# Attention in front of a mixture of experts: row maxima over two PSUM banks, masks written by TensorE, seven PSUM banks dealt out anew

## The reference

```
x1  = layernorm(x)
q, k, v = split(x1 @ W_qkv.T + b_qkv)          # 16 heads, head_dim 8
logits  = where(causal, q @ k.T * 8**-0.5, -inf)
x = x + softmax(logits) @ v @ W_proj.T + b_proj
```

```
z = layernorm(x); top_vals, top_idx = top_k(z @ Wg, 2); gate = softmax(top_vals)
for e in range(8):
    a = gelu(layernorm(z, ln_w[e], ln_b[e]) @ fc1_w[e] + fc1_b[e])
    out += (a @ fc2_w[e] + fc2_b[e]) * comb[:, e]
x = x + out
```

## Time and profile before

| what | value |
|---|---|
| median of three runs | 540.32 us |
| span of the profiled execution | 560.3 us |
| busy: PE, DVE, ACT, POOL | 473.9, 373.1, 322.9, 366.1 us |
| stretch with both passes running | about 40 to 345 us |
| period of one batch in it | 43.1 us (the same rows recur at 173.33, 216.43 and 259.51 us) |
| experts' part | about 368 to 560 us |

### The profile page before, as it was taken

The page is one execution under the profiler, slowest core; times in us unless marked ns, Lnnn a source line. Parts: engine busy times, 40 slices in busy tenths (PEclk is TensorE's granted clock), DMA queues, the critical chain, the costliest instruction groups (busy, mean ns, idle before and its releaser), DMA issues.

```text
span 560.3 us, 11807 instructions
## 1 busy us (share of the span) xinstructions
PE 473.9 (85%) x3296; PEld 277.1 (49%) x3296; DVE 373.1 (67%) x1316; ACT 322.9 (58%) x661; POOL 366.1 (65%) x712
## 2 busy tenths in 40 slices
PE   3379999999999998998898988786992999999930
PEld 1134443543443453443444443364981888888920
DVE  4588878889889889889889997741543521222226
ACT  2137786776676776676676666752550555565610
POOL 5956676586986986987887876955556444445520
PEclk9589999999999999999999999897996899999985
DMA  2323133134233234234224212276642685666439
GB/s 62 93 57 105 65 93 109 58 105 118 68 101 117 78 87 129 73 91 130 75 66 130 71 40 79 79 236 213 219 159 86 213 264 180 216 194 187 154 129 328
DMA packets 52726, 70.83 MB, mean 126 GB/s; under 512 B 11063, under 2 KB 38430, under 8 KB 52662
## 3 DMA queue, kind: packets, MB, share of 16 engines
q1 hardware_dynamic: 47478, 59.19, 34.7%
q0 software_dynamic: 4320, 8.53, 4.5%
q10 hardware_dynamic: 864, 2.36, 1.2%
HBM read 36.49 MB, written 20.94 MB: 102 GB/s over the span
## 4 chain that ended last, share of the span: by engine, by line
PE 51%; DVE 17%; issue 8%; POOL 6%; SPq 5%; DMA 4%; another core or an unknown queue 4%; ACT 3%; ACTq 0%; DVEq 0%; POOLq 0%
PE acc_bank L748 10%; PE slots L739 10%; PE slots L648 7%; PE acc_bank L680 7%; PE slots L665 5%; SPq L496 4%; DVE masked L940 3%; PE misc L616 3%; POOL z_dram L1235 2%; DVE z L893 2%; DVE row_max L934 2%; POOL probs L1252 2%; DMA y_in<-y_dram 2%; PE slots L644 2%
## 5 line engine op out<-in xcount | busy, mean ns | idle before, releaser
L811 ACT ACTIVATE probs<-slots 128x512 f32<-128x512 f32 (+1 forms) x352 | 185.6, 562 | 86.0 <-PE slots L665 79.2
L940 DVE CUSTOM_DVE_ANT_0 masked<-slots,causal_row 128x512 bf16<-128x512 f32 (+1 forms) x256 | 148.9, 614 | 20.8 <-PE slots L648 20.7
L648 PE MATMUL slots<-stack_k,stack_q 125*128 125x256 bf16 (+3 forms) x512 | 128.5, 307 | 19.4 <-DVE row_max L940 7.5
L1252 POOL TENSOR_SCALAR_AFFINE_SELECT probs<-probs 128x128 f32<-128x128 f32 (+2 forms) x352 | 116.1, 350 | 41.3 <-ACT probs L811 37.4
L665 PE MATMUL slots<-stack_q,stack_k 128*128 128x256 bf16 (+3 forms) x512 | 125.6, 301 | 2.9 <-DVE row_max L934 1.5
L1282 POOL DMA_INDIRECT y_dram<-y,z_in x71 | 69.7, 982 | 73.4 <-DVE y L1126 56.8
L841 ACT ACTIVATE hidden<-slots,w_in 128x256 f32<-128x256 f32 (+1 forms) x156 | 63.1, 455 | 82.6 <-PE acc_bank L748 29.2
L680 PE MATMUL acc_bank<-probs,v 128*32 128x512 f32 (+3 forms) x1024 | 95.6, 447 | 3.4 <-POOL probs L1252 2.7
L648 PEld LDWEIGHTS slots<-stack_k,stack_q 125*128 125x128 bf16 x512 | 48.3, 99 | 95.4 <-DVE row_max L940 49.7
L1235 POOL DMA_INDIRECT z_dram<-z,pos x64 | 63.6, 994 | 32.1 <-DVE pos L1034 17.7
L748 PE MATMUL acc_bank<-hidden,w_in 128*128 128x256 f32 (+1 forms) x312 | 73.0, 376 | 7.8 <-issue 4.0
(11 more groups left out here) (168 smaller groups left out, 523.1 us busy)
## 6 DMA issues: line engine op xcount, KB each, us to landing
w_in<-in_wpack SPq DMA_DIRECT2D x39, 516.0 KB
o_dram<-oT SPq DMA_DIRECT2D x32, 256.0 KB, 2.3
stack_k<-parts SPq DMA_DIRECT2D x95, 64.0 KB
stack_q<-parts SPq DMA_DIRECT2D x93, 64.0 KB
z_in<-z_dram SPq DMA_DIRECT2D x32, 132.0 KB
xt<-in_x SPq DMA_DIRECT2D x8, 256.0 KB, 3.7
onT<-o_dram SPq DMA_DIRECT2D x8, 256.0 KB
o_inv<-inv_dram SPq DMA_DIRECT2D x8, 256.0 KB
```

The costliest lines, as they stand in the source:

```text
L648: mm = pe.matmul(cols[:, i, :], q[0:K1, hh, blk * P:blk * P + P], k[0:K1, hh, 0:w], start=len(heads) == 1, stop=True, skip_group_check=True)
L811: act.activation(probs_of(n), columns(n, slot), ACT.Exp, scale=SCALE).then_inc(s_exp, 1)
L940: dve.tensor_tensor_reduce(out=masked[:, n % MASKED, 0:w], in0=slots[:, slot, 0:w], in1=causal_row[:, T - w:T], scale=1.0, scalar=NEG, op0 ...
L1252: pool.affine_select(out=diag, in_=diag, compare_op=ALU.is_ge, fill=0.0, base=0, pattern=[[0, len(heads)], [1, P]], channel_multiplier=-1) ...
```

## The change

**Pass 1** is cut into six pieces per group in place of eleven: two heads of four blocks over two banks (2 x 512 columns) twice, two heads of three blocks over two banks (2 x 384) twice, four heads of two blocks over two banks (2 x 512), and four heads of one block in one bank (512). They stand at ticks 0, 2, 4, 6, 8 and 10. Every piece gets its mask from TensorE and its maxima from one `tensor_reduce`; the fused instruction, its accumulator read and `causal_row` are gone.

**PSUM**: four banks (`scores`) belong to pass 1, used as two pairs; three (`banks`) are a ring that pass 2 and all that was in `misc` share in the order of the list; `acc_bank` stays.

**The probability masks** are cut by GpSimd for two units at once, at ticks 1, 3, 5, 7, 9 and 10 of the unit count, six instructions per group in place of eleven. `probs` has one slot per unit of a group, and exp waits for the p-by-v matmul of the group before.

The core of the diff (renamings of `misc[...]` to `misc(stage)[...]` and of the experts' banks are left out):

The list and the banks:

```diff
+LARGEST = tuple((blocks, tuple(range(h, h + n))) for blocks, n in ((4, 2), (3, 2), (2, 4), (1, 4))
+                for h in range(0, HPG, n))
+SCORED = len(LARGEST)
+SCORE_AT = (0, 2, 4, 6, 8, 10)
+CUT_AT = (1, 3, 5, 7, 9, 10)
+CUT_OF = (2, 4, 5, 6)
...
-SLOTS = 6
+RING = 3
...
-        if n < G * UNITS:
-            add(("pass1", n))
+        g, tick = divmod(n, UNITS)
+        if g < G and tick in SCORE_AT:
+            add(("pass1", SCORED * g + SCORE_AT.index(tick)))
...
+    ring = [s for s in schedule if s[0] == "pass2" or s[0] in MISC]
+    last_pass2 = ring.index(("pass2", G * UNITS - 1))
+    for i, s in enumerate(ring):
+        bank_of[s] = i % RING if i <= last_pass2 else RING - 1
+        used_before[s] = last_use.get(bank_of[s])
+        last_use[bank_of[s]] = s
...
-        slots = ctx.enter_context(nc.psum_tensor("slots", [P, SLOTS, 512], F32))
+        scores = ctx.enter_context(nc.psum_tensor("scores", [P, 4, 512], F32))
+        banks = ctx.enter_context(nc.psum_tensor("banks", [P, RING, 512], F32))
         acc_bank = ctx.enter_context(nc.psum_tensor("acc_bank", [P, 512], F32))
-        misc = ctx.enter_context(nc.psum_tensor("misc", [P, 512], F32))
...
+        def wait_bank(eng, stage):
+
+            before = used_before[stage]
+            if before and before[0] == "pass2":
+                wait(eng, s_exp, before[1] + 1)
+            elif before:
+                wait(eng, s_free, misc_no[before] + 1)
```

TensorE's claim of a bank, its pass 1, and the wait ahead of a p-by-v stage:

```diff
             def claim(stage):
 
-                wait(pe, s_free, misc_no[stage])
+                if stage != ("k", 0):
+                    wait(pe, s_free, misc_no[stage])
+                wait_bank(pe, stage)
...
+            def pass1(m):
+                g, u, w, heads, per_bank = largest_of(m)
                 b, hg = divmod(g, NG)
+                wait(pe, s_max, m - 1)
...
-                if len(heads) > 1:
-                    pe.matmul(cols[:, :, w - P:w], ident_b[:, :], causal[:, 0:len(heads), :],
+                for cols in used:
+                    pe.matmul(cols[:, :, w - P:w], ident_b[:, :], causal[:, 0:per_bank, :],
                               start=True, stop=False, skip_group_check=True)
...
-                last = g * UNITS + ROW_END[row]
-                wait(pe, s_cut, last + 1)
+                wait(pe, s_cut, len(CUT_AT) * g + CUT_OF[row])
```

ScalarE's wait before an exp, VectorE's maxima, and GpSimd's cut:

```diff
-                if n >= P_RING:
-                    old_g, old_u = divmod(n - P_RING, UNITS)
-                    row = NT - UNIT[old_u][0]
-                    wait(act, s_pv, NT * old_g + PV_ORDER.index(row) + 1)
+                if g > 0:
+                    wait(act, s_pv, NT * (g - 1) + PV_ORDER.index(NT - w // P) + 1)
...
-                    dve.tensor_tensor_reduce(out=masked[:, n % MASKED, 0:w], in0=slots[:, slot, 0:w],
-                                             in1=causal_row[:, T - w:T], scale=1.0, scalar=NEG, op0=ALU.add, op1=ALU.max,
-                                             accum_out=largest).then_inc(s_max, 1)
+                used = scores[:, 2 * (m % 2):2 * (m % 2) + len(heads) // per_bank, 0:per_bank * w]
+                if per_bank > 1:
+                    used = used.rearrange("p b (h w) -> p (b h) w", w=w)
+                dve.tensor_reduce(largest, used, AX.X, ALU.max).then_inc(s_max, 1)
...
+                if u not in CUT_AT:
+                    return
                 wait(pool, s_exp, n + 1)
-                diag = probs_of(n)[:, :, 0:P]
+                if len(heads) < HPG:
+                    diag = probs[:, u - 1:u + 1, 0:len(heads) * w]
```

137 lines of the change are left out of this document (64 added, 73 removed).

## The result

Four runs of the changed kernel took 546.7 to 550.75 us, median 548.4; the kernel before beside them 540.61. The ratio is 1.0139 [1.0119, 1.0160], in brackets its 95% interval. Forecast were 536.4 and a range that ended at 546. The profiled execution took 547.7 us with a span of 545.6, so 2 us lie around the span.

A forecast was written before the change was run, and what follows sets the result against it. TensorE bounds the light stretch; in full periods TensorE and VectorE, nearly equal, hold each other up. Periods -6.0, light groups +2.9, first groups -0.9 sum to -4.0, times 0.964 -3.9: 536.4 us; range 526 to 546, the forecast's own 533 to 540.

The forecast's parts named there:

- Masks: Pass 1's two-head pieces: eight added mask matmuls a group at 56 ns, +0.44 us a group, +13.1 us of TensorE's work.
- rival C: Pass 1's masks cost as much as a weight load: 238 x 43 ns = +10, 546 us; chance 0.06.
- Row maxima: VectorE's maxima in pass 1 fall from 6.13 to 5.70 us a group: 0.43 less, 1.7 a batch.
- Cuts: GpSimd's probability cuts fall from 3.86 to 2.90 us a group; the chain to `rstd` ends 0.9 us earlier.
- How PE and DVE mesh: Attention, per batch: TensorE 40.2 us, VectorE 36.8; stalls fall from 4.7 to 1.7, period 41.9, 1.2 less.
- the gaps "by `z`": TensorE's gaps by the layer norm, recorded as 0.22 and 0.17 us, ending with VectorE; 0.2 left as a stall.
- Fill: First two groups, pass 1 alone: VectorE sets the pace, so 2 x 0.43 = -0.9 us; extra masks lie under it.
- the light groups: 6.6 groups ahead of the full periods, all matmuls, no stall to give back: +0.44 us each, +2.9.
- 5.8 periods of -1.2: Batch periods between about 95 and 345 us, the last with a stall less: -6.0 us.
- the factor 0.964: Whole kernel: ratio of the runs' median 540.32 to the profiled 560.3 us; it turns -4.0 into -3.9.
- B: Attention: the ring of three banks makes pass 2 wait for exps or VectorE's reads: +6, 546 us; chance 0.20.
- D: Pass 1: two-bank reductions save nothing, whole pieces are waited for, 2.4 us of stalls stay: 0, 540 us; chance 0.12.

## Why the prediction was wrong, step by step

**Masks.** 56 ns each, 0.44 a light group: measured 0.46 to 0.48 between groups and 44 ns with the masks left out. Right, and rival C is out: neither the price of a weight load nor the 81 ns of the Trainium skill (TensorE: Matmul & The Clock Gate, Back-to-back issue gap) came. They were counted in full in every period, 1.8 us. Put into the kernel before they lengthen it by 0.6, left out of the changed one they give 0.15 back.

**Row maxima.** 36.8 us busy in a period, 1.12 for a piece of 1024: measured 36.86, and three pieces with 3.21 us in all and 0.96 for the last (that is (3.21 - 0.96) / 2 = 1.12 a step). Right.

**Cuts.** 2.90 us a group: 4 x 0.413 + 2 x 0.642 = 2.94. Their value ahead of `rstd` was put at 0.9 and measured at 0.44 and 0.48. That they last longer one by one, and so hold `z` longer, was not seen.

**How PE and DVE mesh: the step that failed.** It said that two engines with equal totals (38.4 and 38.5) hold each other up and that 1.7 us less of VectorE would cut the stalls from 4.7 to 1.7 us of a period, to 41.9. With TensorE's work at the forecast's 40.2 the stalls are 43.46 - 40.2 = 3.3; the recorded idle is 43.40 - 40.89 = 2.5 us, where less than 1.5 was forecast. The totals explain little: halving the maxima frees 9.4 us and gives 1.4, and the kernel before with paired cuts and the moved subtractions keeps its totals on TensorE and VectorE and has a period of 42.06. In the full periods a chain with a few instructions of each engine sets the pace: statistics, GpSimd's root, `z`, its transposes, the top two, gates, dispatches, `rstd`, `xn`. By this account a total on an engine enters only where one of its pieces is a link. And the gaps "by `z`" were put at 0.2 us, while up to 1.3 us of a period lay in that one link, as a lock and not as a dependence, so the chain of waits names VectorE's `z` and no releaser. Moving two instructions of another engine took the recurring period to 42.16, within 0.3 of the forecast with the masks and pieces as they are. That these subtractions hold `z` is shown by the ends of the records and by the runs in which they are shortened or moved; that this sets the period is shown by two of them (shortened, earlier). With the subtractions later, or `z` later, other waits took most of the gain. That the kernel before could have been improved by the same move was overlooked for the same reason.

**Fill.** Forecast -0.9 from VectorE's steps, measured +1.3 and, in the second traces, +1.0. VectorE does set the pace (half maxima bring the first stage to 43.66), but with two-bank pieces its first maximum starts at 23.04 in place of 22.29. That TensorE, with two pairs of banks, then waits for whole pieces is argued; one-bank pieces gave 46.89, and the start with two-bank pieces varies between 46.96 and 49.09 from run to run.

**In sum** the four full periods miss by 6.3 us, the last eight groups by 2.6 and the fill by 2.2, the light groups by -0.5: 10.6 of the 12.0 us between 536.4 and 548.4. The rest would lie behind the last stage of attention, where the forecast had put nothing; it can't be placed, since the trace of before is of an execution 20 us longer. Two slips of the sum matter less. 5.8 periods of -1.2 are -7.0, and it took -6.0 for one stall. And the factor 0.964 spreads those 20 us over the whole kernel, though they lie in the experts' part.

**Rivals.** B had the right side but not the mechanism: TensorE waits 1.0 us in all for exp (L682) in 545, and in a full period of the changed kernel for no bank of the ring. The bank split does harm alone, by a longer wait for `xn` and by the clock, and neither shows in the full change. D, the lateness that stays, was nearest in what it said of the stalls, at a chance of 0.12. Nothing in the list had GpSimd slow VectorE. What cost the groups ahead of the full periods is what was forecast: the masks, +2.9 forecast and +2.4 measured.

## What to carry to other kernels

Before crediting an engine's saved time, find the chain in the stretch and ask which of its instructions get shorter; two totals that are alike prove nothing. Compare the mean durations of one instruction at two places of the kernel: where they differ (344 and 525 ns), look at what GpSimd does in those microseconds. A change that shortens one engine's queue shifts the phase between the queues, so such collisions have to be looked for again after it.

## What the runs showed of the hardware

- Some of VectorE's instructions on SBUF stand until a running GpSimd instruction ends: `tensor_scalar` of 128x128 fp32 (1.10 and 1.20 us for a step of 0.26) and `tensor_tensor` of 128x4 with both inputs in SBUF (1.12 for 0.08). Others do not: statistics (0.28 to 0.29) and the search for the top values (`MAX8`, 0.15 to 0.16) last no longer inside a subtraction. `xn` inside a dispatch (`z_dram`) took 0.62 us in the changed kernel and ended 0.02 after it. Reductions from PSUM are not held up to the end of a subtraction either: each record beside one is 1.23 us or less for 1024 columns, as elsewhere.
- After TensorE stood 2.40 us, and once after 2.08, its granted clock was 0.50 for some 3.4 us; after 1.07 us, after 1.55 in the kernel with single cuts and after 1.80 in the one with moved subtractions and paired cuts it stayed at 1.00. In the run without masks it was 0.50 once from 292.6 us, with no wait above 1.07 in the 7 us before.
- A `tensor_reduce` over two PSUM banks costs 1.216 us for 1024 columns, 0.950 for 768 and 0.691 for 512 (pieces of one bank): 1.01 and 1.04 ns a column, no price for the second bank.
- One program, the kernel before, differed by 4% from time to time (541.57 and 562.30 us, both on a chip numbered 3). In the traces of long and short executions the difference lies behind attention, where weights come from HBM.
